# Two spreads of a field's ids from two 32-row groups of the array (DLRM tower, one core)

## What is computed

```python
e = jnp.stack([tbl_0[ids[:, 0]], ..., tbl_25[ids[:, 25]]], axis=1)      # (512, 26, 128)
combined = jnp.concatenate([e, r_dense_x[:, None, :]], axis=1)          # (512, 27, 128)
z = jnp.einsum('bfd,bgd->bfg', combined, combined)[:, TRIU_I, TRIU_J]   # pairs f < g
h = jnp.concatenate([z, r_dense_x], axis=1)                             # (512, 479)
h = jnp.maximum(h @ W_top1 + b_top1, 0.0)                               # 512 wide
h = jnp.maximum(h @ W_top2 + b_top2, 0.0)                               # 256 wide
y = h @ W_top3                                                          # (512, 1)
```

## Time and profile before

| | us |
|---|---|
| median of 3 runs | 112.58 |
| the three runs | 110.67, 112.70, 112.58 |
| profiled execution, whole time | 110.61 |
| its span | 108.80 |
| PE, DVE, ACT, POOL busy in the span | 101.8, 80.2, 75.4, 62.8 |

### The profile page before, as it was taken

One profiled execution on the slowest core, in us unless ns is written; L12 is line 12 of the kernel. 1 busy time (PEld: TensorE's weight loads), 2 busy tenths in 40 slices (PEclk: granted clock), 3 DMA queues, 4 the chain that ended last, 5 costly groups with the idle time before them and its releaser, 6 DMA issues.

```text
span 108.8 us, 2593 instructions
## 1 busy us (share of the span) xinstructions
PE 101.8 (94%) x994; PEld 79.9 (73%) x994; DVE 80.2 (74%) x161; ACT 75.4 (69%) x148; POOL 62.8 (58%) x72
## 2 busy tenths in 40 slices
PE   5999999989999999999898977999999989799992
PEld 1447567655766656688577967999999979798991
DVE  5599999979999999999972783489337932386210
ACT  4599379999999999999945762376527732376320
POOL 3777777777777777776777777777776000000000
PEclk9999999999999999999999999999999999999999
DMA  2854649994563817551112222122221100000000
GB/s 45 336 200 69 227 90 409 369 304 78 214 182 116 256 39 262 125 215 48 48 48 60 66 54 48 48 54 65 60 50 48 30 0 0 6 0 0 0 6 1
DMA packets 5199, 11.64 MB, mean 107 GB/s; under 512 B 1978, under 2 KB 2490, under 8 KB 5188
## 3 DMA queue, kind: packets, MB, share of 16 engines
q1 hardware_dynamic: 3120, 7.27, 20.2%
q0 software_dynamic: 2048, 4.20, 14.6%
q10 hardware_dynamic: 20, 0.02, 0.1%
HBM read 11.48 MB, written 0.00 MB: 106 GB/s over the span
## 4 chain that ended last, share of the span: by engine, by line
PE 89%; DVE 5%; issue 2%; ACT 1%; DVEq 0%
PE gram_ps L556 39%; PE gram_ps L591 13%; PE tr_ps L572 6%; PE act_ps L625 5%; PE dve_ps L625 4%; PE top_ps L636 3%; PE tr_ps L673 3%; DVE pairs L470 2%; PE dve_ps L532 2%; PE tr_ps L667 2%; PE gram_ps L532 2%; PE top_ps L660 2%; PE gram_ps L612 1%; PE tr_ps L625 1%; PE act_ps L532 1%
## 5 line engine op out<-in xcount | busy, mean ns | idle before, releaser
L280 POOL DMA_INDIRECT rows<-table,ids_sb x64 | 61.9, 967 | 20.7 <-issue 19.2
L556 PE MATMUL gram_ps<-onehot,high 128*128 128x512 f32 x82 | 23.2, 429 | 1.0 <-issue 1.0
L556 PE MATMUL gram_ps<-onehot,low 128*128 128x512 f32 x82 | 21.4, 404 | 0.0
L556 PEld LDWEIGHTS gram_ps<-onehot,high 128*128 128x128 f32 x82 | 15.3, 201 | 7.4 <-issue 3.6
L556 PEld LDWEIGHTS gram_ps<-onehot,low 128*128 128x128 f32 x82 | 14.7, 188 | 6.1 <-issue 3.4
L294 ACT ACTIVATE xt<-gram_ps 128x512 f32<-128x512 f32 x10 | 12.0, 1202 | 4.9 <-PE gram_ps L556 4.9
L591 PE MATMUL gram_ps<-xt 128*58 128x52 f32 x512 | 14.5, 217 | 0.9 <-DVE xt L429 0.6
L443 DVE TENSOR_TENSOR onehot<-dve_ps,row_f 128x1024 fp32r<-128x1024 f32 (+1 forms) x10 | 14.4, 1484 | 1.2 <-PE act_ps L532 1.2
L591 PEld LDWEIGHTS gram_ps<-xt 128*58 128x58 f32 x512 | 14.0, 133 | 1.6 <-DVE xt L429 0.8
L455 DVE TENSOR_TENSOR low<-table,high 128x256 fp32r<-128x256 f32 (+1 forms) x40 | 14.5, 426 | 0.8 <-ACT high L372 0.6
L443 DVE TENSOR_TENSOR onehot<-gram_ps,row_f 128x1536 fp32r<-128x1536 f32 (+1 forms) x10 | 14.9, 1536 | 0.0
(11 more groups left out here) (72 smaller groups left out, 106.5 us busy)
## 6 DMA issues: line engine op xcount, KB each, us to landing
table<-table SPq DMA_DIRECT2D x9, 512.0 KB, 3.9
rows<-table,ids_sb POOLq DMA_INDIRECT x64, 3.0
w1p_sb<-w_pairs SPq DMA_DIRECT2D x1, 768.0 KB, 5.6
table<-table SPq DMA_DIRECT2D x1, 640.0 KB, 4.1
w_sb<-w SPq DMA_DIRECT2D x1, 512.0 KB, 7.0
dense_sb<-dense SPq DMA_DIRECT2D x1, 256.0 KB, 4.9
w1d_sb<-w_dense SPq DMA_DIRECT2D x1, 256.0 KB, 5.9
ids_sb<-ids SPq DMA_DIRECT2D x1, 52.0 KB, 1.9
```

The lines of the kernel that those rows point to most:

```text
L280: pool.indirect_dma_start(rows[:, t, s - 1, :], None, tables[f], bass.IndirectOffsetOnAxis(ids_sb[:, t, f:f + 1], 0)).then_inc(gathered[t] ...
L556: last = pe.matmul(pick_ps[b][:], weights[:, c, :], onehot[:, b, c, :], start=(c == 0 and part == 0), stop=(c == CHUNKS[o] - 1 and part == 1))
```

## The change

The ids and the selection are kept twice, in partitions 0 to 9 and in partitions 32 to 41. The first matmul of a spread takes both operands from the former, the second from the latter. For this `field_of`, `field_ids`, `field_ids16` and `select` grow from 10 to 42 partitions, the host lays the ids out in 42 rows (rows 10 to 31 are zeros), and a third iota writes the field numbers for partitions 32 to 41, offset by 32 so that the comparison with the row number selects there too. Its partitions overlap no other iota's; it waits for the two before, the identity waits for it, and VectorE's first copy waits for all three.

```diff
+SPREAD_AT = (0, 32)
+SPREAD_ROWS = 32 + NO
...
-        field_of = sb("field_of", [NO, NO], I32)
+        field_of = sb("field_of", [SPREAD_ROWS, NO], I32)
...
-        field_ids = sb("field_ids", [NO, B], I32)
-        field_ids16 = sb("field_ids16", [NO, B], F16)
-        select = sb("select", [NO, NO, P], F16)
+        field_ids = sb("field_ids", [SPREAD_ROWS, B], I32)
+        field_ids16 = sb("field_ids16", [SPREAD_ROWS, B], F16)
+        select = sb("select", [SPREAD_ROWS, NO, P], F16)
...
-            pool.iota(field_of[:], pattern=[[1, NO]], base=0, channel_multiplier=0).then_inc(row_ready, 1)
+            pool.iota(field_of[0:SPREAD_AT[1]], pattern=[[1, NO]], base=0, channel_multiplier=0).then_inc(row_ready, 1)
             pool.iota(row_of[:], pattern=[[P, MAX_CHUNKS]], base=0, channel_multiplier=1).then_inc(row_ready, 1)
             pool.wait_ge(ident_zero, 1)
+            pool.wait_ge(row_ready, 2)
+            pool.iota(field_of[SPREAD_AT[1]:], pattern=[[1, NO]], base=SPREAD_AT[1], channel_multiplier=0
+                      ).then_inc(row_ready, 1)
+            pool.wait_ge(row_ready, 3)
...
-            dve.wait_ge(row_ready, 2)
+            dve.wait_ge(row_ready, 3)
...
             dve.tensor_scalar(select[:], field_of[:].rearrange("k (o p) -> k o p", p=1
-                                                               ).to_broadcast([NO, NO, P]),
-                              row_f[0:NO, 0:1], None, ALU.is_equal).then_inc(select_ready, 1)
+                                                               ).to_broadcast([SPREAD_ROWS, NO, P]),
+                              row_f[0:SPREAD_ROWS, 0:1], None, ALU.is_equal).then_inc(select_ready, 1)
...
-                for ps in (ids_ps_dve[o % 2], ids_ps_act[o % 2]):
-                    last = pe.matmul(ps[:], select[:, o, :], field_ids16[:], start=True, stop=True)
+                for at, ps in zip(SPREAD_AT, (ids_ps_dve[o % 2], ids_ps_act[o % 2])):
+                    last = pe.matmul(ps[:], select[at:at + NO, o, :], field_ids16[at:at + NO, :], start=True, stop=True)
                 last.then_inc(ids_spread, 1)
...
+    ids_by_field = np.zeros((SPREAD_ROWS, B), a["ids"].dtype)
+    for at in SPREAD_AT:
+        ids_by_field[at:at + NO] = a["ids"].reshape(Q, G, TILES, N_FIELDS).transpose(3, 2, 1, 0).reshape(N_FIELDS, B)[ONEHOT]
```

More of the change, by code:

```diff
@@ L755 @@
         "ids": a["ids"],
-        "ids_by_field": np.ascontiguousarray(
-            a["ids"].reshape(Q, G, TILES, N_FIELDS).transpose(3, 2, 1, 0).reshape(N_FIELDS, B)[ONEHOT]),
+        "ids_by_field": ids_by_field,
         "w1_pairs": w1_pairs,
```

## The result

| | before | changed |
|---|---|---|
| median, us | 111.62 (4 runs) | 109.25 (4 runs) |
| lowest and highest, us | 110.67, 112.70 | 109.23, 109.52 |
| profiled execution, us | 110.61 | 109.23 |
| its span, us | 108.80 | 107.40 |

The ratio is 0.9877, with a 95% interval of 0.9851 to 0.9903. It counts only the executions near each kernel's fastest, for the kernel before the two at 110.67, because that kernel runs on several levels; these levels are what the rest of this document is about.

What follows compares the result with a forecast made beforehand. TensorE bounds the start, ScalarE the fields, TensorE the end. Pair savings of 0.35 and 0.37 less 0.2 for the load, plus the third spread, taken as 0.55, bring 110.61 to 110.06, so 110.1; range 109.2 to 112.8.

Steps and rivals of the forecast that it cites:

- the first spread at 3.2 to 3.5: Sign of being right at TensorE's start: first spread starts at 3.2 to 3.5 us, against 3.09 before.
- the first copy 0.5 to 0.8 earlier: Sign of being right on ScalarE: its first copy of a pick starts 0.5 to 0.8 us before 14.29.
- The pair: Two matmuls of each of ten spreads on TensorE: starts 0.03 us apart, saving 2.3 us of its time in all.
- The join out of the spread: From a spread into the next pick on TensorE: stays 0.31 us, with no third join inside the pair.
- the two reasons given: For 0.03 us inside a spread: results go to different banks; both weight loads are out before the first matmul is under way.
- The load: Ids load at the start, 10 to 42 rows: conversion and first spread 0.2 us later, bounds 0 and 0.6.
- The iota: One more on GpSimd before VectorE's first copy: 0.15 us with its wait, bounds 0.1 and 0.3; costs nothing to 0.15.
- if the rise moves with the work, it is worth 0.52: TensorE's start: 0.52 us of slow work saved counts fully if the clock's rise moves along, 0.27 if its time stays.
- Rival D: First pick's high part: clock rises earlier, up to eight matmuls at fast spacing, 1.8 us off the forecast, 108.3; chance 0.10.
- The fields: From 14.29 to 52.8 us ScalarE sets the pace, 4.55 per field; the seven later spreads' 1.3 us add nothing.
- Rival A: TensorE bounds the fields too; all 2.3 us less the start's 0.2 come out: 108.5; chance 0.07.
- C: Clock rises later, after the first low part: eight matmuls cost 1.8 us more, 111.9; a second burst, 113.7; chance 0.21.

Runs made afterwards that it cites:

- the doubled pair: Changed kernel with the second spread's side-by-side pair issued twice into the same banks; six runs: 109.10, 109.11, 109.12, 109.13, 110.81, 111.38 us.
- the moved spread: Kernel before (10 rows, nothing side by side) with the second spread moved ahead of the three later warm-up matmuls; median 109.88 us, four runs from 109.43 to 109.94.

## Why the prediction was right, and where it was not

The time lay in the stated range and, by the ratio, within 2%; the forecast of 110.1 was 0.85 above the median, which lies 0.05 inside the lower end of the range. That is partly luck: of the 1.53 us by which ScalarE's first copy came earlier, 1.15 is the early rise of the clock in the first pick, which the sum did not hold. Two of the signs of being right failed, the first spread at 3.2 to 3.5 (it was 3.78) and the first copy 0.5 to 0.8 earlier. Point by point:

- **The pair** (taken 0.03 apart, bounds 0.03 and no gain): 0.002 to 0.006 us in the trace, 0.01 as the rows print it. The join out of the spread is still 14.79 - 14.48 = 0.31, and no third one came. The Trainium skill, TensorE: Matmul & The Clock Gate, Part 3, gives about 4 ns, and TensorEngine Tiling (Array Packing), section Key Properties, lets only a change of mode drain the array; these distances agree with both. One of the two reasons given does not stand: in the kernel before, the second load of weights starts with or just behind the first matmul (3.09 and 3.09, 6.90 and 6.89), not ahead of it. No run tests the reasons apart.
- **The load** (taken 0.2, bounds 0 and 0.6): 0.68, past the upper bound. That bound was the landing of the 52 KB of all ids, which is no bound for a load of 84 KB; and beside the larger load those ids came later too (the first gather at 3.64). The iota, with its waits, cost about 0.2 (selection at 1.70 for 1.51, taken 0.15), hidden behind the load. The first spread is 0.69 late, which eats what the first two pairs save, 0.38 + 0.40, but for 0.12 at the first pick. This is the term that was mis-sized most. With it, the same sum gives about 0.25 in place of 0.55 (0.35 + 0.37 - 0.69 = 0.03 in the first two pairs, 0.2 to 0.25 in the third).
- **The rise of the clock.** The step "if the rise moves with the work, it is worth 0.52" treated the rise as fixed, at the same time or at the same work. It is neither: it is drawn anew in each execution, from about 8 to 16 us in these traces. Rival D, at a chance of 0.10, is what the profiled pair shows, while the reason that I gave it (the picks come earlier) is not the reason found. That the two levels seen lie a later rise apart held (the second trace of the kernel before, 2.0 us). But I laid the profiled execution beside the lower of two; there are three, and it was on the middle one.
- **The fields** (the seven later savings add nothing): held. ScalarE's field stayed at 4.55 to 4.60, and with eight pairs serial again the median moved by 0.1 to 0.2, the best run not at all. Rival A is out. What I didn't see is that VectorE, once ScalarE starts early enough, is the next bound from the very start, and that the late load then costs it 0.29 directly.
- **The sign by which C and D were to be told**, eight picks at another spacing, was the right one to look at.

So the change does two things. It costs about 0.2 us where the clock rises early anyway (changed 109.07 to 109.34, before 108.99 to 109.01 at its best, same chip). And it takes the two upper levels away, where 50 of all 64 runs of the kernel before lay. Shown by runs: with the second spread side by side, none of 44 runs (five kernels, two of them run twice) lay above 110.4; with it serial in its old place, these 50 of 64, 4 of 10, 4 of 4 and 3 of 6 did. The traces agree: the clock rises between about 8 and 10.5 us in the seven with it side by side, and between about 8 and 16 in the five with it serial in its old place. That it is the length of this interruption between warm-up and first pick (from the spread's start to the pick's, 7.84 - 6.89 = 0.95 us before and 7.72 - 7.18 = 0.54 changed), rather than the two running at once, rests on the doubled pair (2 of 6) and on the moved spread (0 of 4): likely, by few runs. Left open is whether the later start alone raises the share of early runs (14 of 64 in the kernel before; 6 of 10, 0 of 4 and 3 of 6 in the three kernels with a late start and a serial second spread), and what ties the rise to the program beyond that.

## What to carry to other kernels

Where a kernel's runs lie on levels, take several traces before comparing two: look for the place where equal matmuls change their spacing, and ask whether a change moves the levels or only which of them are met. A change may be worth little in the stage that it was counted in and still 2 us or more in the median (111.62 to 109.25 in the first comparison, 112.59 to 109.18 in the last), most likely because it shortens an interruption before the clock has risen. And when an operand is needed in two copies, the first use should not wait for the load of the second.

## What was not expected of the hardware

In one program, the kernel before, the clock of TensorE rose at about 11.7 us in one execution and at about 16 in another; over all these kernels it rose between about 8 and 16 us. TensorE was at work from 1.19 us on, with one wait of up to 0.71 us before the first spread. Equal 512-column matmuls were 0.43 us apart until the rise, the lower of its two levels (1.2 GHz), and 0.23 after, the upper (2.4 GHz). The page's clock row shows 9 from the first slice in all of these profiles, so it can't be used for it. With the second pair serial, 0.95 us from its start to the first pick at the lower level, early and late rises both came; with it side by side, 0.54 us, the latest was at about 10.5. A load of 42 rows of 2 KB let the conversion start at 3.04 to 3.22 over the traces, one of 10 rows alone on the same queue at 2.44 to 2.55, 0.5 to 0.8 us earlier. Beside the larger load, the 52 KB of all ids on another queue took 2.4 to 2.6 us from issue to landing instead of 1.8 to 2.0.
